# Attention stage of a convolution, attention and feed-forward kernel: rows of maxima issued by GpSimd, maxima of three heads in one instruction, another order on TensorE, loop written out

## What is computed

```python
x = x + conv_ref(_gn(x), weight_coord, radius, weights)   # depthwise 11x11, kernels built from 4 points
t = _to_tokens(x)                                         # 16 x 256 tokens x 96
t = t + attn_ref(_ln_t(t), w_attn, w_proj)
t = t + ffn_ref(_ln_t(t), W1, b1, W2, b2)                 # sign-binarised weights, groups of 3 images
x = _from_tokens(t, x)

def attn_ref(x, w_attn, w_proj):                          # 6 heads of 16
    q, k, v = jnp.split(x @ w_attn, 3, axis=-1)           # then split in heads
    q = _apply_rope(q, emb); k = _apply_rope(k, emb)
    wei = jnp.einsum('bhqd,bhkd->bhqk', q, k) * scale
    wei = jnp.where(causal[None, None], wei, -jnp.inf)
    wei = jax.nn.softmax(wei, axis=-1)
    out = jnp.einsum('bhqk,bhkd->bhqd', wei, v)
    return out.transpose(0, 2, 1, 3).reshape(B, T, C) @ w_proj
```

## Time and profile before

| | |
|---|---|
| median of 3 runs | 310.63 us (309.91 to 310.65) |
| profiled execution | 311.95 us |
| its span, first to last instruction | 310.2 us |
| mean granted clock of TensorE in it | 0.936 |
| busy: PE / PEld / DVE / ACT / POOL | 247.3 / 188.1 / 209.0 / 154.5 / 112.5 us |
| DMA | 15.62 MB in 25849 packets |

### The profile page before, as it was taken

One profiled execution on the slowest core, in us unless ns is written; L12 is line 12 of the kernel. 1 busy time (PEld: TensorE's weight loads), 2 busy tenths in 40 slices (PEclk: granted clock), 3 DMA queues, 4 the chain that ended last, 5 costly groups with the idle time before them and its releaser, 6 DMA issues.

```text
span 310.2 us, 6132 instructions
## 1 busy us (share of the span) xinstructions
PE 247.3 (80%) x1880; PEld 188.1 (61%) x1880; DVE 209.0 (67%) x646; ACT 154.5 (50%) x349; POOL 112.5 (36%) x117
## 2 busy tenths in 40 slices
PE   0239898999999786799877889899877969788881
PEld 0129898898889564568666667676444535454440
DVE  1898538778775899757766657776367574756454
ACT  0520444546545434456655656666765754545350
POOL 1560544567556723622322322332786040000000
PEclk9999999999999977589999999999999969795978
DMA  4900000000199300334334345330000010101011
GB/s 126 266 6 0 27 25 25 3 25 29 51 126 116 40 0 3 77 73 87 77 81 94 87 106 97 77 77 1 2 1 0 2 33 5 38 1 38 2 52 38
DMA packets 25849, 15.62 MB, mean 50 GB/s; under 512 B 3873, under 2 KB 25697, under 8 KB 25825
## 3 DMA queue, kind: packets, MB, share of 16 engines
q1 hardware_dynamic: 23568, 14.04, 23.4%
q10 hardware_dynamic: 2256, 1.29, 1.8%
HBM read 4.26 MB, written 1.57 MB: 19 GB/s over the span
## 4 chain that ended last, share of the span: by engine, by line
PE 47%; SPq 17%; DVE 16%; issue 8%; ACT 4%; DMA 4%; POOL 2%; DVEq 0%; ACTq 0%; POOLq 0%
SPq L373 12%; PE bank L1205 10%; PE bank L1453 8%; PE bank L1468 7%; PE bank L1231 4%; SPq L389 4%; DVE parts L1103 3%; DVE qr_ring L906 3%; PE bank L1220 3%; DMA stack<-nmax_t 2%; PE bank L1346 2%; DMA rad_bc<-in_L_conv_radius 2%; DVE rest_ring L880 2%; PE bank L1304 2%; PE bank L1321 1%
## 5 line engine op out<-in xcount | busy, mean ns | idle before, releaser
L955 DVE TENSOR_REDUCE nmax<-bank 128x1 f32<-128x128 f32 x192 | 55.0, 349 | 29.0 <-PE bank L1307 28.6
L489 POOL TENSOR_SCALAR_AFFINE_SELECT pt_ring<-pt_ring 128x512 f32<-128x512 f32 x48 | 31.0, 645 | 67.2 <-ACT pt_ring L657 67.1
L657 ACT ACTIVATE pt_ring<-bank 128x384 f32<-128x384 f32 x96 | 41.7, 487 | 22.4 <-PE bank L1323 21.8
L1205 PE MATMUL bank<-xs_ring,toep 128*128 128x192 f32 x256 | 49.2, 337 | 0.6 <-issue 0.6
L1205 PEld LDWEIGHTS bank<-xs_ring,toep 128*128 128x128 f32 x256 | 43.6, 197 | 2.2 <-issue 0.9
L1304 PE MATMUL bank<-stack 96*128 96x128 bf16 x192 | 34.8, 257 | 1.7 <-DVE nmax L955 1.3
L1307 PE MATMUL bank<-mask,ident 128*128 128x128 bf16 x192 | 34.7, 228 | 0.0
L1321 PE MATMUL bank<-stack 97*128 97x256 bf16 x96 | 23.3, 287 | 12.8 <-DMA stack<-nmax_t 9.6
L460 POOL TENSOR_TENSOR parts<-rest_ring,parts 96x512 bf16<-96x512 f32 x16 | 25.4, 1590 | 21.8 <-DVE parts L883 21.8
L1453 PE MATMUL bank<-parts,w_b 96*128 96x384 f32 x60 | 27.1, 599 | 0.0
L1068 DVE TENSOR_REDUCE amax<-parts 128x1 f32<-128x384 f32 x30 | 16.4, 552 | 15.8 <-ACT parts L712 14.7
(11 more groups left out here) (151 smaller groups left out, 488.2 us busy)
## 6 DMA issues: line engine op xcount, KB each, us to landing
stack<-parts SPq DMA_DIRECT2D x96, 96.0 KB, 3.4
x_ring<-in_x SPq DMA_DIRECT2D x8, 192.0 KB, 2.4
out<-xs_ring SPq DMA_DIRECT2D x5, 288.0 KB, 2.6
stack<-in_x SPq DMA_DIRECT2D x2, 384.0 KB, 6.7
stack<-in_x ACTq DMA_DIRECT2D x2, 384.0 KB, 10.8
stack<-nmax_t SPq DMA_DIRECT2D x32, 1.5 KB
cst<-in_const SPq DMA_DIRECT2D x1, 384.0 KB, 11.7
w_in<-in_L_ffn_W ACTq DMA_DIRECT2D x2, 144.0 KB, 12.0
```

The lines of the kernel that those rows point to most:

```text
L489: nc.gpsimd.affine_select(out=v, in_=v, compare_op=ALU.is_ge, fill=0.0, base=0, pattern=[[0, 2], [0, 2], [1, P]], channel_multiplier=-1).t ...
L657: nc.scalar.activation(pt_ring[:, s, h, :], bank[:, 3 + h % 2, 0:T + P], ACT.Exp, scale=float(HD) ** -0.5).then_inc(s_exp, 1)
L955: last = nc.vector.tensor_reduce(nmax[:, n0 % 2, HEADS * t + h:HEADS * t + h + 1], bank[:, h % 3, first:first + (t + 1) * P], op=ALU.max, ...
L1205: nc.tensor.matmul(dst, w, xs_ring[:, s, p, k].rearrange("p b c -> p (b c)"), start=(k == 0 and p == 0), stop=False)
```

## The change

- `max_row` moves from SyncE to GpSimd: the two DMAs of batch n + 1 are issued in GpSimd's step n between its first and its second select; the row of batch 0 goes between its last work of the stage before. SyncE keeps only the images, and waits for the second scores of batch n - 6, the last user of the slot, instead of n - 5.
- `maxima` covers three heads (banks 0 to 2) in one instruction of 128x384 and one of 128x768 elements; `s_max` counts groups of three, and `scores_q` of three heads waits for the group before.
- TensorE's order in step n: `scores_k` pair 0; three heads of `scores_q(n + 2)`; `scores_k` pair 1; `transpose_max(n + 1)`; `weighted_values(n - 1)`; `transpose_norm(n - 2)`; three heads; `scores_k` pair 2; `project_out(n - 2)`; `transpose_o(n - 1)`. The transposed maxima go to bank 5 instead of bank 2.
- ScalarE: the middle two exponentials come right behind `max_out`, then the copies in the order `o_ring`, `ot_ring`, `v_ring`, then the last two exponentials. VectorE: reciprocal and product of batch n - 2 first in its step (before: of n - 1 inside it), then six maxima in two groups, then addition and statistics of n - 2.
- The loop is written out: `BB` has no laps, and all steps have constant counts.
- In the steps in front of the loop the maxima and `scores_q` are regrouped in threes as well.

```diff
-        BB = dict(start=2, first=2, unroll=RING, laps=2, last=B - 2)
+        BB = dict(start=2, first=B - 2, unroll=1, laps=0, last=B - 2)
...
-                wait(sp, s_sk, HEADS * (b - RING + 2))
...
-            for n in range(4):
-                stack_ready(0, n)
+                wait(sp, s_sk, HEADS * (b - RING + 1))
+
+            for n in range(B):
+                stack_ready(n)
                 stack_image(0, n)
-            max_row(0, 0)
-
-            def step_b(i, n0):
-                max_row(i, n0 - 3)
-                stack_ready(i, n0)
-                stack_image(i, n0)
-            run(sp, step_b, start=4, first=4, unroll=RING, laps=2, last=B)
...
+            def max_row(n0):
+
+                slot = n0 % RING
+                pool.wait_ge(s_mtc, n0 + 1)
+                for t in range(NT):
+                    nc.gpsimd.dma_start(stack[KROWS:KROWS + 1, slot, :, 0, t * P:(t + 1) * P],
+                                     nmax_t[t * HEADS:(t + 1) * HEADS, n0 % 2, :]).then_inc(s_mrow[slot], 16)
+
             def step_b(i, n0):
                 for hp in range(3):
+                    if hp == 1 and n0 + 1 < B:
+                        max_row(n0 + 1)
...
             sines(0, PAIRS - 1, 1)
+            max_row(0)
             third(0, PAIRS - 2, 1)
...
                     exps(0)
                 if n0 + 1 < B:
                     max_out(i, n0 + 1)
+                if n0 < B:
+                    exps(1)
+                if 1 <= n0 <= B:
+
+                    wait(act, s_pv, b)
+                    wait(act, s_otr, b - 2)
+                    nc.scalar.copy(o_ring[:, 1 - s, :], bank[0:C, 7, :]).then_inc(s_o, 1)
...
-            def maxima(i, n0, h):
+            def maxima(i, n0, g):
...
-                dve.wait_ge(s_sq, HEADS * b + h + 1)
-                if h == 0:
+                dve.wait_ge(s_sq, HEADS * b + 3 * (g + 1))
+                if g == 0:
                     wait(dve, s_mt, b - 1)
                 for t in range(NT):
-                    first = t * P
-                    last = nc.vector.tensor_reduce(nmax[:, n0 % 2, HEADS * t + h:HEADS * t + h + 1],
-                                                   bank[:, h % 3, first:first + (t + 1) * P],
+                    first, k = t * P, HEADS * t + 3 * g
+                    last = nc.vector.tensor_reduce(nmax[:, n0 % 2, k:k + 3], bank[:, 0:3, first:first + (t + 1) * P],
                                                    op=ALU.max, axis=AX.X, negate=True)
...
             def step_b(i, n0):
-                b = n0 + RING * i
+                if 2 <= n0 <= B + 1:
+                    normalise_o(i, n0 - 2)
                 if n0 + 2 < B:
-                    for h in range(4):
-                        maxima(i, n0 + 2, h)
+                    maxima(i, n0 + 2, 0)
+                    maxima(i, n0 + 2, 1)
                 if n0 >= 2:
...
+                    add_attention(i, n0 - 2)
...
-                wait(pe, s_max, HEADS * b + h - 2)
-                if h == 2:
-
-                    wait(pe, s_mtc, b)
+                if h % 3 == 0:
+                    wait(pe, s_max, 2 * b + h // 3)
...
             def step_b(i, n0):
...
+                if n0 < B:
+                    scores_k(i, n0, 0)
+                if n0 + 2 < B:
+                    scores_three(i, n0 + 2, 0)
+                if n0 < B:
+                    scores_k(i, n0, 1)
+                if n0 + 1 < B:
+                    transpose_max(i, n0 + 1)
+                if 1 <= n0 <= B:
+                    weighted_values(i, n0 - 1)
+                if n0 >= 2:
+                    transpose_norm(i, n0 - 2)
+                if n0 + 2 < B:
+                    scores_three(i, n0 + 2, 1)
+                if n0 < B:
+                    scores_k(i, n0, 2)
+                if n0 >= 2:
+                    project_out(i, n0 - 2)
+                if 1 <= n0 <= B:
+                    transpose_o(i, n0 - 1)
```

More of the change, by code:

```diff
@@ L977, in second_stats, with normalise_o @@
                                         ALU.add).then_inc(s_l2var, 1)
+            def normalise_o(i, n0):
+                b = n0 + RING * i
+                dve.wait_ge(s_otr, b + 1)
+                o = bank[:, 5, 0:4 * C].rearrange("p (n k) -> p n k", k=2 * HD)
+                nc.vector.reciprocal(rsum[:], o[:, :, HD]).then_inc(s_rsum, 1)
+                dve.wait_ge(s_rsum, b + 1)
+                wait(dve, s_ont, b)
+                nc.vector.tensor_tensor(o_norm[:].rearrange("p t (h d) -> p (t h) d", d=HD), o[:, :, 0:HD],
+                                        rsum[:].unsqueeze(2).broadcast_to([P, NT * HEADS, HD]),
+                                        ALU.mult).then_inc(s_on, 1)
@@ new lines, in add_attention @@
+            def add_attention(i, n0):
+                b = n0 + RING * i
+                dve.wait_ge(s_proj, b + 1)
+                t_b = tok[:, ds(b, 1), :, :].rearrange("p o t c -> p (o t) c")
+                nc.vector.tensor_tensor(t_b, bank[:, 6, T:T + NT * C].rearrange("p (t c) -> p t c", t=NT), t_b,
+                                        ALU.add).then_inc(s_res, 1)
+                wait_apart(dve, s_res, b + 1)
+                for t in range(NT):
+                    last = nc.vector.bn_stats(
+                        ln2_st[:, ds(2 * b + t, 1), :].rearrange("p o k -> p (o k)"),
+                        tok[:, ds(b, 1), t, :].rearrange("p o c -> p (o c)"))
+                last.then_inc(s_l2st, 1)
@@ L990, in step_b @@
-                if 1 <= n0 <= B:
-                    dve.wait_ge(s_otr, b)
-                    o = bank[:, 5, 0:4 * C].rearrange("p (n k) -> p n k", k=2 * HD)
-                    nc.vector.reciprocal(rsum[:], o[:, :, HD]).then_inc(s_rsum, 1)
-                if n0 + 2 < B:
-                    for h in range(4, HEADS):
-                        maxima(i, n0 + 2, h)
-                if 1 <= n0 <= B:
-                    dve.wait_ge(s_rsum, b)
-                    wait(dve, s_ont, b - 1)
-                    nc.vector.tensor_tensor(o_norm[:].rearrange("p t (h d) -> p (t h) d", d=HD), o[:, :, 0:HD],
-                                            rsum[:].unsqueeze(2).broadcast_to([P, NT * HEADS, HD]),
-                                            ALU.mult).then_inc(s_on, 1)
@@ L1029, in _ @@
             rotate(0, PAIRS - 1, 0)
-            for h in range(3, HEADS):
-                maxima(0, 1, h)
+            maxima(0, 1, 1)
             dve.wait_ge(s_wps, 1)
@@ L1357, in transpose_o @@
                 wait(pe, s_on, b)
+                if n0 + 2 < B:
+                    wait(pe, s_mtc, b + 3)
                 for t in range(NT):
```

92 lines of the change are left out of this document (26 added, 66 removed).

## The result

| | before | after |
|---|---|---|
| median | 310.27 us (308.48 to 310.65) | 316.44 us (315.88 to 316.62) |
| span of the profiled execution | 310.2 us | 314.1 us |
| its mean granted clock | 0.936 | 0.918 |

The changed kernel is slower: 1.0207 times the time of before, with a 95% interval of 1.0164 to 1.025. The forecast of 305.7 us had the wrong sign, and 316.44 lies above its range. (Medians are over all executions. Ratios leave out those that ran in a slower state of the chip, so they need not equal the quotient of two medians.)

The account below looks back on a forecast made before the run. The prediction took SyncE's queue, issuing images and rows of maxima at some 6.3 us a batch, as the bound. Its sum was 310.6 - 7.3 (loop) + 0 (front) + 2.4 (tail) = 305.7 us, range 302 to 315.5.

Parts of the forecast that it names:

- (1): SyncE's queue in the loop: without the rows its period falls to about 4.7 us and it sets nothing.
- (2): TensorE's work in a loop batch: 5.44 us in the new order, with nothing removed from the sum.
- (3): VectorE's maxima: three heads in two instructions take 1.41 us, saving 0.4 us a batch.
- The ring: Loop between VectorE and TensorE: grouped maxima, VectorE's small work, maxima again, then three heads of scores; 5.4 us.
- (4): Row of maxima through GpSimd in the loop: sets a period of 5.75 us, 7.3 us less over 13 batches.
- D: Time for the two row issues and their landing: taken as 3.62 us on GpSimd, 3.1 on SyncE.
- The forecast's own sign of being wrong: Rows through GpSimd: a landing over 2.8 us after the second issue began would show the forecast wrong.
- Rival C: Loop: the row's chain becomes what SyncE's queue was, making the kernel slower, from D = 4.0 with period 6.1; chance 0.22.
- (5): Front, up to batch 2: grouped maxima save VectorE time against longer waits; zero, from -2 to +2 us.
- (6): Tail: o_norm of the last batch moves behind the first hidden half's maxima; costs 2.4 us, between 0.5 and 3.5.
- rival E: Front: TensorE's new waits in batches 0 and 1 prolong the lower clock, +3 us on the forecast; chance 0.08.
- (7): Written-out loop: register steps and branches go, priced at zero as hidden; at most 0.1 us a batch.

Follow-up runs that it names:

- c4_all_per_head: c3 with the maxima taken head by head again instead of three heads together; 310.0 us, 0.985 of before.
- a3: The changed kernel with the first second_stats moved behind VectorE's step 14; 313.6 us, 1.014 of before.
- a1: The changed kernel with the transposed maxima in bank 3 instead of bank 5, without the wait for o_norm; 313.4 us, 1.010 of before.
- f1_no_images: c3 without the stack images of batches 6 to 15, the rows of maxima still sent; 304.2 us (one execution).
- c3: The changed kernel with the edits of a1, a2_tail and a3 together; 308.5 us, 0.981 of before.
- a2_tail: The changed kernel with o_norm of the last batch taken ahead of the maxima of the first hidden half; 310.0 us, 1.002 of before.
- e1: The changed kernel with only the grouped maxima undone, each head's maxima by themselves again; 313.7 us, 1.011 of before.
- b2_flat: The kernel before with the loop over the batches written out, SyncE's own loop kept; 311.9 us, 1.000 of before.
- b3: The kernel before with both loops written out, SyncE's too, and the exact slot wait, rows of maxima still on SyncE; 305.5 us, 0.982 of before.
- c5: c3 with the rows of maxima back on SyncE's written-out queue; 305.0 us, 0.982 of before.
- b1: The kernel before with the rows of maxima on GpSimd, the exact slot wait and both loops written out; 307.6 us, 0.990 of before.

## Why the prediction was wrong

In the two traces the forecast was 8.8 us too low: it had 4.9 us less, and the stretches give 3.9 more. The thirteen batches from k0(2) to k0(15) lack 6.5 of that (7.3 less forecast, 0.8 less measured), the tail 2.4; the rest is +0.8 behind the clip and -0.9 ahead of k0(2).

- (1) SyncE off the chain: right.
- (2) TensorE's sum of 5.44 us a batch: right, 5.42 where nothing else held it (c4_all_per_head). The sum named the work but not its waits: the transposed maxima now wait for o_norm, which the diff showed (`wait(pe, s_on, b - 2)`) and my working never priced. In the loop it costs nothing beside the late rows; in step 14, where `second_stats(0)` stood ahead of o_norm, the step fell by 2.6 to 3.1 us once it was gone (a3, a1), of which 1.4 are the clock's. This is the first failed step.
- (3) Maxima of three heads: 1.41 forecast, 1.43 measured. The ring was mis-sized: 5.4 forecast, 5.71 measured (f1_no_images). I had it run through VectorE's small work and the maxima; it runs through the maxima and TensorE's in-order list between the two groups. Grouping lengthens the floor by 0.29 us (5.42 in c4 to 5.71 in f1 and c3) where I had it save 0.4 of VectorE's time.
- (4) D, forecast 3.62. GpSimd's issue was priced too high, 0.53 us and not 1.04. The flight was mis-sized the other way, and this is the second failed step: 1.54 us taken from the end of the second issue, 2.2 to 3.5 measured on the chain while images fly (2.7 to 4.0 from its start, less the issue). The 0.28 us from ScalarE's copy to the first issue stood in no term. D was 3.5 to 4.8 there, against 3.62; that it came so near is luck, two errors of opposite sign. I had taken the flight, read from a row that SyncE issued behind its images, as a property of the transfer; f1 shows that GpSimd's, issued while images are issued, depends on the traffic. The loop gave 3.7 us in twelve batches, where 7.3 were expected in thirteen. The forecast's own sign of being wrong, a landing over 2.8 us after the second issue began, came. Rival C had the sign and, in part, the mechanism: at its point of decision, D = 4.0, it had a period of 6.1, and 6.09 was measured. But it had the tail eat that gain, and the loss came as much from the wait in (2) and from the clock, which it didn't have.
- (5) Front: +1.3 us from k0(0) to k0(2), within the -2 to +2. Kernels with the same front differ by more (16.59 in a3_stats, 14.41 in a2_tail, at a granted clock of 0.55 and 0.76 from 120 to 134 us), so its sign is not shown. Both halves of the term did show: grouping alone (after against e1, c3 against c4) brings k0(0) 1.8 to 1.9 us forward in these two pairs, and makes the step from k0(0) to k0(1) 1.0 longer.
- (6) Tail: 2.4 forecast, 4.8 measured, beyond its end of 3.5. The mechanism was right, o_norm behind the hidden maxima, and so was its size: counted from k0(15) the transposes came 2.4 us later (2.0 forecast), and with the product at the full clock the order costs 2.2 in all (a3). a2 gives back 4.4 by moving it alone. The failed term is the one that was not there: in this execution TensorE's idle 1.79 us was followed by the lower clock, and six products went from 2.13 to 4.10 us. That such a fall could come I priced for the front (rival E) and not for the tail.
- (7) Written-out loop, priced at zero: right for TensorE and its neighbours (b2_flat), wrong for SyncE, the engine that set the period. Its register steps were 0.54 us a batch. The cover I named, "the sequencer's lead", is one that a queue on the chain doesn't have. This is where the gain of the loop could be had without the rest of the change.

Summed from the stretches: -2.1 + 1.3 - 3.7 + 2.9 + 4.8 + 0.8 = +3.9 us, the difference of the spans. The medians differ by 6.2: the profiled execution of before took 311.95 us, 1.7 above its median, and that of after 315.88, 0.6 below, so the remaining 2.2 us is in no stretch.

## What to carry to other kernels

When a loop's period is a queue's, look at the gaps between its issues first: written out, SyncE's loop gave here 1.6 to 1.8% that the larger rebuilding gave only after three mends. A row that must arrive just in time got no faster here on another engine's queue as long as the bulk traffic flew beside it. And after every reordering, walk each wait that changed its partner through the first and last steps, where other work is interleaved: steady state hid both of the waits that made this change slower. Read such a step from the start of the step before it, and not by absolute times, or what was gained earlier hides the loss.

## What the runs showed of the hardware that I had not expected

- A 1.5 KB DMA issued by GpSimd cost that engine 0.53 us (mean), less than SyncE's 0.74 (median) for the same transfer, and landed in 1.7 us (median, from the issue) in quiet and 3.0 beside the images of 96 KB.
- The Trainium skill, "DMA: Bandwidth & Descriptors", section "Latency and other measured facts", gives about 1 us to the first byte for GpSimd and about 0.6 for SyncE, 0.4 apart. No run here shows the first byte. The profile's chains do have some flights of SyncE's rows: 2.28 and 2.29 us from the start of the second issue in before, 2.22 in b3, 1.75 and 2.68 in c5, against 2.7 to 4.2 for GpSimd's in after and b1 while images fly. SyncE never issues a row while it issues an image, GpSimd does; whether the queue or the moment of the issue makes the difference, no run separates. By time, the kernels with rows on either don't differ beyond their intervals (0.990 and 0.982 in b1 and b3, 0.981 and 0.982 in c3 and c5).
- TensorE's idle 1.79 us ahead of L1364 was followed by a granted clock of 0.51 from 232 to 240 us; with the idle time moved (a2), 229 to 237 us had 1.00. But a3, with the same idle time, still had 1.00 for the product behind it, so one idle time of this length doesn't settle when the clock falls. What did, in each execution, stays open.
